# First layer of a two-layer graph network: number row and phases in PSUM, node sums added behind the keys, ScalarE's products first in its turn, and the rounding of the angles on ScalarE

## The chip, the cores and the metric

The kernel runs on one core of a Trainium2 chip. The metric is the device time of one execution in microseconds (us). The kernel before takes 9845.34 us, the median of three runs.

## What is computed

Two message-passing layers over 12500 nodes of 128 channels and 400000 edges, sorted by their target node. Cut to what matters here, the first layer is:

```python
rel_t = last_update[src] - t
rel_t_enc = cos(rel_t[:, None] * time_w[None, :] + time_b)     # 32 phases per edge
e = (concat([rel_t_enc, msg]) @ We)                            # 96 -> 128, two heads of 64
alpha = sum(q_all[dst] * (k_all[src] + e), per head) / 8
ex = exp(alpha - segment_max(alpha, dst)[dst])
out = segment_sum((v_all[src] + e) * ex / segment_sum(ex), dst) + x @ Wskip + bskip
x = layernorm(x + out)
```

The second layer sums `edge_weight * x[src]` per target node, multiplies by a matrix and normalizes again. The change does not touch it.

## The kernel before

Edges come in tiles of 128, one per partition. The first layer walks them in 880 *steps* of G = 4 tiles. Every engine runs its own instruction stream, a loop over *turns*: in turn k an engine does a fixed list of *stages*, each for a step that lies ahead by a fixed number. `(ve_stage, 14)` in the list means that turn k does the `ve` work of step k + 14. The order of that list is the order on the engine, written by hand in each `body`; semaphores tie the engines together. Eight turns are a *round*: once per round come the stages that `first_of` guards (the running maximum over the edges of a node). Counted within a round, turn 3 has the forward and backward scan, turn 4 the running maxima and `new`, turn 5 `shift` and the exponentials, turn 6 `keep`. An angle is worked on for two steps at once (BATCH = 2), in the even turns.

One step passes these stages, in this order:

- GpSimd (POOL) gathers keys, values and update time of 512 source nodes (L817) and subtracts the edge times (`rel`, L825).
- ScalarE (ACT), `arg_stage` (L1178): four products of the phases' frequencies with `rel`, written into `feat`.
- VectorE (DVE), `angle(0)` (L1503) adds the phase offsets; `angle(1)` (L1506) adds MAGIC = 12582912, which rounds to a whole number; `angle(2)` (L1508) subtracts it. Then ACT's `sine_stage` (L1167).
- TensorE (PE), `feat_stage` (L955) transposes `feat`; ACT's `featc_stage` (L1161) copies it out of PSUM; PE's `e_stage` (L963) multiplies with `We`.
- DVE, `ve_stage` (L1518) and `ke_stage` (L1523) add `e` to values and keys; `onehotT_stage` (L1530); PE's `q_stage` (L973); DVE's `product_stage` (L1537) and `alpha_stage` (L1544).
- Once per round: PE transposes alpha (L992), DVE scans forward (L1576) and backward (L1583), PE's `small_stage` (L1006) spreads the ends and ACT's `smallc_stage` (L1194) copies them; DVE takes running maxima (L1602 to L1627) and `new` (L1635), PE's `newT_stage` (L1015) transposes it back, DVE's `shift_stage` (L1642) subtracts, ACT's `exp_stage` (L1201) and `dropx_stage` (L1208) exponentiate, DVE's `keep_part` (L1650 to L1658) ends the round.
- ACT, `weigh_stage` (L1154): eight scaled copies of the values; DVE, `onehot_stage` (L1559), compares the target nodes with the row of numbers 0 to 127 (`irow`); PE's `sum_stage` (L982) sums by node; DVE's `sum_stage` (L1670) adds to `acc`.

Before, `agg_ps`, the target of PE's `sum_stage`, has two banks. ACT alternates between two function tables, one for the sine and one for the exponential, so it loads a table twice a round.

Of the kernel before, what the change touches and what calls it, by code (L numbers as in the profile page):

```python
# [49 lines left out]
def build(nc, x, src, dst, attr, weight, node_vec, time_w, time_b, Wq, bq, Wk, bk, Wv, bv, We, Wskip, bskip, W1, b1, out):  # L50
# [36 lines left out]
    with ctx:  # L87
# [3 lines left out]
        def sem(name):  # L91
            return ctx.enter_context(nc.semaphore(name))
# [25 lines left out]
        eps = sb("eps", [P, 1])  # L118
        We1 = sb("We1", [TD + MSG, C])
# [185 lines left out]
        agg_ps = [banks[6 + j][:, 0:HEADS * HB] for j in range(2)]  # L305
        irow_ps, one_ps = banks[7][:, 0:P], banks[7][0:NB, P:P + 1]
        RANKS = SEGMENT * P
# [40 lines left out]
        s_rows0 = sems("s_rows0", 2)  # L348
# [10 lines left out]
        ANG = 3  # L359
# [516 lines left out]
        def _(pe):  # L876
# [99 lines left out]
            def sum_stage(st):  # L976

                pe.wait_ge(s_wv, st.s + 1)
                pe.wait_ge(s_oh, st.s + 1)
                wait(pe, s_acc, st.before(2))  # L980
                for g in range(G):
                    op = pe.matmul(agg_ps[st.k % 2], oh[:, st.k % QS, g, :], wv[:, st.k % 2, g, :, :].rearrange("p h c -> p (h c)"),  # L982
                                   start=(g == 0), stop=(g == G - 1))
                op.then_inc(s_agg, 1)
# [33 lines left out]
            def body(i):  # L1018
                for k in range(UNROLL0):
                    if first_of(k, 5, ROUND):  # L1020
                        at(i, k, (alphaT_stage, 5))
                    at(i, k, (feat_stage, 15), (sum_stage, 1), (q_stage, 14), (e_stage, 15))
                    if first_of(k, 5, ROUND):
                        at(i, k, (small_stage, 5))
                    if first_of(k, 4, ROUND):
                        at(i, k, (newT_stage, 4))
# [92 lines left out]
        def _(act):  # L1119
# [42 lines left out]

            def sine_stage(st):

                act.wait_ge(s_ang, ANG * (st.batch() + 1))
                enc = encodings(st)
                act.activation(enc, enc, ACT.Sin, bias=zero[:, :], scale=-2.0 * PI_BELOW).then_inc(s_enc, 1)  # L1167

            EDGES, group1 = {0: 6, 6: 8, 14: 2}, {}
# [40 lines left out]
            def body(i):  # L1210
                for k in range(UNROLL0):
                    if k in EDGES:
                        groups_stage(mybir.EngineType.Activation, group1, Step(i, k + 18), EDGES[k])
                    sines = [(sine_stage, 16)] if k % BATCH == 0 else []
# [3 lines left out]
                    at(i, k, (featc_stage, 15), (weigh_stage, 2), *sines, (arg_stage, 18), *gaps, *exps, *smalls)  # L1218
# [74 lines left out]
        def _(dve):  # L1293
# [7 lines left out]
            dve.memset(eps[:, :], 1e-5)  # L1301
            dve.memset(run[:, :, :], -BIG)
# [187 lines left out]
            dve.memset(acc[:, :], 0.0)  # L1490


            def angle(n):

                def stage_of(st):
                    a, t = encodings(st), turns[:, :, :]
                    done = ANG * st.batch()
                    if n:
                        dve.wait_ge(s_ang, done + n)
                    else:  # L1500
                        dve.wait_ge(s_arg, st.s + BATCH)
                    if n == 0:
                        op = dve.tensor_tensor(a, a, brow[:, :].unsqueeze(1).to_broadcast([P, BATCH * G, TD]), ALU.add)  # L1503
                    elif n == 1:
                        wait(dve, s_ang, done)
                        op = dve.tensor_scalar(t, a, MAGIC, None, ALU.add)  # L1506
# [49 lines left out]
            def onehot_stage(st):  # L1556
                dve.wait_ge(s_rel0, st.round() + 1)
                wait(dve, s_agg, st.before(QS))
                dve.tensor_tensor(oh[:, st.k % QS, :, :], irow[:, :].unsqueeze(1).to_broadcast([P, G, P]),  # L1559
# [120 lines left out]
            def body(i):  # L1680
                for k in range(UNROLL0):
# [4 lines left out]
                    def once(ahead, *stages):  # L1686
                        return [(stage_of, ahead) for stage_of in stages] if first_of(k, ahead, ROUND) else []

                    at(i, k, *turn[0], (ve_stage, 14), *turn[1], (ke_stage, 14), *turn[2], (block_stage, 0), *once(5, forward_stage),
                       (onehotT_stage, 15), *once(5, backward_stage), (product_stage, 13), *once(4, run_stage, first_stage),  # L1690
                       (onehot_stage, 2), *once(11, rel0_stage), *once(4, col_stage, drop_stage), (alpha_stage, 13), *once(4, new_stage), *once(3, shift_stage),
                       (sum_stage, 0), *once(8, pen_stage), *once(2, keep_part(0), keep_part(1), keep_part(2)))
# [251 lines left out]
```

## Time and profile before

| | |
|---|---|
| median of three runs | 9845.34 us (9844.81 to 9847.26) |
| the profiled execution, its time and its span | 9864.48 us, 9862.8 us |
| span: VectorE, TensorE, GpSimd, ScalarE busy | 87%, 77%, 68%, 52% |
| first layer's loop, one stretch of 300 us: VectorE, TensorE, ScalarE, GpSimd | 276.31, 233.70, 229.49, 221.06 us |
| steps of the first layer in 800 us (3000 to 3800 us) | 150 |

The times under an engine are those in which it executed an instruction. Consecutive instructions on DVE and ACT overlap by some 0.06 to 0.10 us in the records: what one costs its engine is the distance from its start to the next start, not its duration.

### The profile page before, as it was taken

What the parts mean: (1) busy time and instruction counts of PE and PEld (TensorE: products, weight loads), DVE (VectorE), ACT (ScalarE), POOL (GpSimd) and SP (SyncE); (2) the same over time, 40 slices, a digit from 0 to 9 for tenths busy, and PEclk for the clock granted to TensorE, in tenths of its full rate; (3) what the DMA queues carried; (4) which work ended last, traced back from release to release, by engine and by line L of the source; (5) the groups of instructions that cost most, each with busy time, mean ns of one, the idle gap of its engine ahead of it and who ended that gap; (6) DMA issues with size and microseconds to landing.
All of it is one profiled execution on the core that took longest, in us unless ns stands there. A gap on an engine that the chain in (4) does not pass through costs nothing.

```text
span 9862.8 us, 272152 instructions
## 1 busy us (share of the span) xinstructions
PE 7624.6 (77%) x52868; PEld 7101.3 (72%) x52869; DVE 8560.3 (87%) x21301; ACT 5115.0 (52%) x20838; POOL 6708.6 (68%) x6871
## 2 busy tenths in 40 slices
PE   6477777777777777777756777788888888888855
PEld 2477777777777777777756777787888877877754
DVE  5899999999999999999987666799999999999968
ACT  2377777777777777777753333333333333333300
POOL 0477777777777777777745777777777777777720
PEclk8688988888888888898875555688888888888888
DMA  6467666676666666666632222355555555555544
GB/s 191 114 180 178 179 177 177 178 179 178 176 177 180 177 176 177 178 181 177 177 97 69 71 71 71 106 151 147 149 147 149 148 148 149 148 148 149 148 133 116
DMA packets 1631706, 1484.67 MB, mean 151 GB/s; under 512 B 792007, under 2 KB 1363043, under 8 KB 1631203
## 3 DMA queue, kind: packets, MB, share of 16 engines
q1 hardware_dynamic: 1374244, 848.34, 34.3%
q0 software_dynamic: 257088, 632.95, 22.8%
q14 instruction: 335, 2.74, 0.1%
q8 instruction: 39, 0.64, 0.0%
HBM read 1225.51 MB, written 254.87 MB: 150 GB/s over the span
## 4 chain that ended last, share of the span: by engine, by line
issue 25%; DVE 19%; POOL 18%; PE 14%; DMA 7%; ACT 7%; DVEq 6%; SPq 3%; ACTq 2%; POOLq 0%
POOL message_scratch L869 17%; DMA message_scratch<-ohT,idx 6%; PE bank L982 3%; DVE y_all L1537 3%; PE bank L973 3%; ACT arena L1154 2%; DVEq L531 2%; PE bank L955 2%; PE bank L1015 2%; PE bank L963 2%; DVE acc L1670 1%; SPq L728 1%; DVE oh L1583 1%; DVE oh L1576 1%; DVE kve L1523 1%
## 5 line engine op out<-in xcount | busy, mean ns | idle before, releaser
L817 POOL DMA_INDIRECT kv<-kv_scratch,arena x3136 | 3265.7, 1041 | 1236.6 <-issue 837.5
L869 POOL DMA_INDIRECT message_scratch<-ohT,idx x3232 | 3214.2, 994 | 1079.0 <-issue 880.2
L1261 ACT ACTIVATE ohT<-bank,kv 128x128 f32<-128x128 f32 x3232 | 923.9, 369 | 2703.8 <-DMA message_scratch<-ohT,idx 2665.1
L1154 ACT ACTIVATE arena<-arena,weights 128x65 f32<-128x65 f32 x7040 | 1771.6, 337 | 2.4 <-PE bank L982 2.3
L1063 PE MATMUL bank<-acc,oh 128*128 x6464 | 1211.2, 345 | 520.3 <-ACT ohT L1262 514.4
L1063 PEld LDWEIGHTS bank<-acc,oh 128*128 128x128 f32 x6464 | 1054.7, 247 | 627.7 <-issue 625.2
L1077 PE MATMUL bank<-oh,kve 128*128 128x128 f32 x8640 | 1387.7, 321 | 144.7 <-DVE arena L1838 107.8
L982 PE MATMUL bank<-arena,oh 128*128 128x130 f32 x7040 | 1164.1, 318 | 280.8 <-DVE acc L1670 274.8
L1077 PEld LDWEIGHTS bank<-oh,kve 128*128 128x128 f32 x8640 | 1248.0, 227 | 167.8 <-issue 157.3
L982 PEld LDWEIGHTS bank<-arena,oh 128*128 128x128 f32 x7040 | 1048.2, 227 | 362.6 <-issue 295.1
L973 PE MATMUL bank<-arena,ohT 128*128 128x128 f32 x7040 | 1090.6, 306 | 0.0
L973 PEld LDWEIGHTS bank<-arena,ohT 128*128 128x128 f32 x7040 | 1031.3, 225 | 0.3 <-issue 0.2
L1161 ACT ACTIVATE featT<-bank 96x512 f32<-96x512 f32 x880 | 518.3, 589 | 917.0 <-PE bank L955 895.0
L963 PE MATMUL bank<-We,featT 96*128 96x128 f32 x7040 | 979.5, 284 | 18.3 <-ACT featT L1161 18.3
L963 PEld LDWEIGHTS bank<-We,featT 96*128 96x128 f32 x7040 | 914.3, 202 | 21.4 <-ACT featT L1161 20.1
L1178 ACT ACTIVATE feat<-wrow,rel 128x32 f32<-128x32 f32 x3520 | 830.6, 308 | 163.7 <-POOL rel L825 161.2
L1769 DVE TENSOR_TENSOR_SCAN y_all<-bank,y_all,kv 98x512 f32<-98x512 f32 x707 | 900.4, 1274 | 0.2
L955 PE MATMUL bank<-ident,feat 128*96 128x128 f32 x3520 | 610.7, 301 | 311.9 <-ACT feat L1167 297.5
L1828 DVE TENSOR_TENSOR oh<-bank,kv 128x768 f32<-128x768 f32 x720 | 689.5, 958 | 76.3 <-DVE kv L1821 37.5
L1518 DVE TENSOR_TENSOR arena<-kv,bank 128x512 f32<-128x512 f32 x880 | 597.9, 679 | 159.2 <-PE bank L963 103.6
L1045 PEld LDWEIGHTS bank<-ones,featT 98*128 98x128 f32 x3232 | 516.9, 242 | 226.6 <-issue 173.5
L1794 DVE TENSOR_SCALAR oh<-bank,icol 128x512 f32<-128x512 f32 x808 | 605.5, 749 | 74.5 <-issue 35.5
(232 smaller groups left out, 12653.6 us busy)
## 6 DMA issues: line engine op xcount, KB each, us to landing
kve<-message_scratch SPq DMA_DIRECT2D x2160, 129.0 KB
kve<-nodes_scratch SPq DMA_DIRECT2D x880, 256.0 KB
feat<-in_edge_attr_dram SPq DMA_DIRECT2D x880, 96.0 KB
feat<-block_scratch SPq DMA_DIRECT2D x812, 98.0 KB
arena<-q_scratch SPq DMA_DIRECT2D x880, 64.0 KB
message_scratch<-ohT,idx POOLq DMA_INDIRECT x3232
kv<-kv_scratch,arena POOLq DMA_INDIRECT x3136
feat<-in_edge_attr_dram SPq DMA_DIRECT2D x880, 32.0 KB
```

Source lines behind the costliest of these rows:

```text
L817: pool.indirect_dma_start(kv[:, k, g, :], None, kv_d, bass.IndirectOffsetOnAxis(ap=group_rows[:, half, k * G + g, 0:1].bitcast(I32), axis= ...
L869: pool.indirect_dma_start(msg_d, bass.IndirectOffsetOnAxis(ap=idx[:, k, g:g + 1], axis=0), sum_ring[:, k % RING1, g, :], None).then_inc(s_ ...
L955: op = pe.transpose(featT_ps[:, g * P:(g + 1) * P], feat[:, k, g, :], ident[:, :])
L963: op = pe.matmul(e_ps[st.k % 2][:, g * P:(g + 1) * P], featT[:, st.k % 2, g * P:(g + 1) * P], We1[:, :], start=True, stop=True)
L973: op = pe.matmul(q_ps[st.k % 2][:, g * P:(g + 1) * P], ohT[:, r, g * P:(g + 1) * P], qb[:, r, :], start=True, stop=True)
L982: op = pe.matmul(agg_ps[st.k % 2], oh[:, st.k % QS, g, :], wv[:, st.k % 2, g, :, :].rearrange("p h c -> p (h c)"), start=(g == 0), stop=(g ...
L1063: op = pe.matmul(banks[2 + st.k % 2][:, g * P:(g + 1) * P], oht1[:, st.k % RING1, g * P:(g + 1) * P], acc[:, bass.ds(places[g], C)], start ...
L1077: op = pe.matmul(banks[4 + sg.half][:, b * P:(b + 1) * P], mt[:, sg.slot(MT) + b, a, 0:C], seg_oh[:, sg.half, b, a, :], start=(a == 0), st ...
L1154: op = act.activation(wv[:, st.k % 2, g, h, :], vR[:, st.k, g, h, :], ACT.Copy, scale=weights[:, st.k // ROUND, g, st.k % ROUND, h:h + 1])
L1178: op = act.activation(feat[:, k, g, 0:TD], wrow[:, :], ACT.Copy, scale=of[:, g:g + 1])
L1261: act.activation(sum_ring[:, st.k % RING1, g, 0:C], banks[2 + st.k % 2][:, g * P:(g + 1) * P], ACT.Copy, scale=taken[:, st.k, g, 2:3])
L1769: dve.tensor_tensor_scan(ranks[0:NB, st.k % 2, :], one_ps.to_broadcast([NB, G * P]), in_blk[0:NB, st.k % 2, :], since, ALU.mult, ALU.add). ...
```

## The change

Five things, all in the first layer's loop:

1. `irow` and the phase offsets `brow` are copied once into PSUM bank 7 and read from there by `onehot_stage` and `angle(0)`.
2. `angle(1)` leaves DVE. ACT does it, in a new `whole_stage` with bias MAGIC. ANG, the count of DVE's angle stages, is 2.
3. ACT's turn begins with `arg_stage`, for step k + 17 where it was k + 18 at the end; then `whole_stage`, `featc_stage` and the rest. The stages of a round stay at the end of the turn.
4. DVE's `sum_stage` moves from the end of its turn to behind `ke_stage`, the last angle stage behind it, the scans one place back.
5. Both halves of `agg_ps` are now in bank 6, so PE's `sum_stage` waits until DVE has added the previous step, and it moves to the end of PE's turn.

```diff
-        agg_ps = [banks[6 + j][:, 0:HEADS * HB] for j in range(2)]
+        agg_ps = [banks[6][:, j * HEADS * HB:(j + 1) * HEADS * HB] for j in range(2)]
+        brow_ps = banks[7][:, P:P + TD]
...
-        ANG = 3
+        ANG = 2
...
# TensorE
-                wait(pe, s_acc, st.before(2))
+                wait(pe, s_acc, st.s)
...
-                    at(i, k, (feat_stage, 15), (sum_stage, 1), (q_stage, 14), (e_stage, 15))
+                    at(i, k, (feat_stage, 15), (q_stage, 14), (e_stage, 15), (sum_stage, 1))
...
# ScalarE
+            def whole_stage(st):
+                act.wait_ge(s_ang, ANG * st.batch() + 1)
+                act.activation(turns[:, :, :], encodings(st), ACT.Identity, bias=magic[:, :]).then_inc(s_whole, 1)
...
-                    at(i, k, (featc_stage, 15), (weigh_stage, 2), *sines, (arg_stage, 18), *gaps, *exps, *smalls)
+                    at(i, k, (arg_stage, 17), *wholes, (featc_stage, 15), (weigh_stage, 2), *sines, *gaps, *exps, *smalls)
...
# VectorE
+            dve.tensor_copy(irow_ps, irow[:, :])
+            dve.tensor_copy(brow_ps, brow[:, :]).then_inc(s_tab, 1)
...
                     if n:
-                        dve.wait_ge(s_ang, done + n)
+                        dve.wait_ge(s_whole, st.batch() + 1)
                     else:
                         dve.wait_ge(s_arg, st.s + BATCH)
                     if n == 0:
-                        op = dve.tensor_tensor(a, a, brow[:, :].unsqueeze(1).to_broadcast([P, BATCH * G, TD]), ALU.add)
-                    elif n == 1:
-                        wait(dve, s_ang, done)
-                        op = dve.tensor_scalar(t, a, MAGIC, None, ALU.add)
+                        op = dve.tensor_tensor(a, a, brow_ps.unsqueeze(1).to_broadcast([P, BATCH * G, TD]), ALU.add)
...
-                dve.tensor_tensor(oh[:, st.k % QS, :, :], irow[:, :].unsqueeze(1).to_broadcast([P, G, P]),
+                dve.tensor_tensor(oh[:, st.k % QS, :, :], irow_ps.unsqueeze(1).to_broadcast([P, G, P]),
...
-                    at(i, k, *turn[0], (ve_stage, 14), *turn[1], (ke_stage, 14), *turn[2], (block_stage, 0), *once(5, forward_stage),
-                       (onehotT_stage, 15), *once(5, backward_stage), (product_stage, 13), *once(4, run_stage, first_stage),
+                    at(i, k, *turn[0], (ve_stage, 14), (block_stage, 0), (ke_stage, 14), (sum_stage, 0), *turn[1],
+                       (onehotT_stage, 15), *once(5, forward_stage), (product_stage, 13), *once(5, backward_stage), *once(4, run_stage, first_stage),
...
-                       (sum_stage, 0), *once(8, pen_stage), *once(2, keep_part(0), keep_part(1), keep_part(2)))
+                       *once(8, pen_stage), *once(2, keep_part(0), keep_part(1), keep_part(2)))
```

How the streams move is seen best at two places on ACT and one on DVE. First ACT at the end of turn 5 of a round, before: the last of the four products (L1178), then the wait for DVE's `shift`, the exponentials, and the copy of the next turn.

```order
L1178 ACTIVATE feat<-wrow,rel 128x32
L366 REGISTER_ALU [waits s_shift]
L1201 ACT_TABLE_LOAD
L1201 ACTIVATE weights<-shifted,zero 128x64 [waits s_wv]
L366 REGISTER_ALU [waits s_drop]
L1208 ACTIVATE drop<-drop,zero 128x16 [waits s_keep]
L517 ISA
L517 TENSOR_LOAD walk_rows
L1159 REGISTER_ALU
L1161 ACTIVATE featT<-bank 96x512 [waits s_e,s_feat]
```

The same place now (the products' line is L1185, the exponentials' L1208 and L1215): behind the exponentials comes the first of the four products of turn 6.

```order
L368 REGISTER_ALU [waits s_shift]
L1208 ACT_TABLE_LOAD
L1208 ACTIVATE weights<-shifted,zero 128x64 [waits s_wv]
L368 REGISTER_ALU [waits s_drop]
L1215 ACTIVATE drop<-drop,zero 128x16 [waits s_keep]
L1181 REGISTER_ALU
L1185 REGISTER_ALU [waits s_feat,s_rel]
L1185 REGISTER_ALU
L1185 ISA
L1185 ACTIVATE feat<-wrow,rel 128x32
```

What moved: the products that DVE's next `angle(0)` waits for (semaphore `s_arg`) stood ahead of the wait for `s_shift` and of the table load, and now stand behind both. ACT at the end of turn 3, before: a product, then the copy of the scans' ends.

```order
L1178 ACTIVATE feat<-wrow,rel 128x32
L1194 ACTIVATE small<-bank 128x64 [waits s_first,s_small]
L1159 REGISTER_ALU
L1161 ACTIVATE featT<-bank 96x512 [waits s_e,s_feat]
L1150 REGISTER_ALU [waits s_ex]
L1154 ACTIVATE arena<-arena,weights 128x65 [waits s_agg,s_kve]
```

And now:

```order
L1156 ACTIVATE arena<-arena,weights 128x65 x7
L1201 ACTIVATE small<-bank 128x64 [waits s_first,s_small]
L1181 REGISTER_ALU
L1185 REGISTER_ALU [waits s_feat,s_rel]
L1185 REGISTER_ALU
L1185 ISA
L1185 ACTIVATE feat<-wrow,rel 128x32
```

What moved: the products of turn 4 now follow the copy that waits for PE (`s_small`), which itself waits for DVE's backward scan. DVE at the start of turn 6, before (L1503 to L1523 are the angles, values and keys):

```order
L1503 TENSOR_TENSOR feat<-feat,brow 128x8x32 [waits s_arg]
L366 REGISTER_ALU
L1517 REGISTER_ALU [waits s_wv]
L1518 REGISTER_ALU [waits s_e]
L1518 REGISTER_ALU
L1518 ISA
L1518 TENSOR_TENSOR arena<-kv,bank 128x8x64
L1499 ISA
L1506 TENSOR_SCALAR arena<-feat 128x256 [waits s_ang]
L1523 ISA [waits s_prod]
L1523 TENSOR_TENSOR kve<-kv,bank 128x512
```

And now, from the values on (L1526 values, L1531 keys, L1678 the node sums, L1516 the last angle stage; ahead of it L1514, `angle(0)`, is still first and still waits for `s_arg`):

```order
L1526 TENSOR_TENSOR arena<-kv,bank 128x8x64
L533 ISA
L533 TENSOR_LOAD walk_rows
L1531 ISA [waits s_prod]
L1531 TENSOR_TENSOR kve<-kv,bank 128x512
L1673 REGISTER_ALU
L1678 ISA [waits s_acc,s_keep,s_agg]
L1678 SCALAR_TENSOR_TENSOR acc<-acc,keep,bank 128x65
L1678 ISA
L1678 SCALAR_TENSOR_TENSOR acc<-acc,keep,bank 128x65
L1510 REGISTER_ALU
L1516 SCALAR_TENSOR_TENSOR feat<-arena,feat 128x8x32 [waits s_whole]
```

What moved: the rounding (L1506) is gone, the two node sums stand behind the keys, and the last angle stage behind them.

## Rows read from the trace of the kernel before

**Rows 1.** The page: span, busy times, and the group of the value stage

```profile
span 9862.8 us, 272152 instructions
...
PE 7624.6 (77%) x52868; PEld 7101.3 (72%) x52869; DVE 8560.3 (87%) x21301; ACT 5115.0 (52%) x20838; POOL 6708.6 (68%) x6871
...
L1518 DVE TENSOR_TENSOR arena<-kv,bank 128x512 f32<-128x512 f32 x880 | 597.9, 679 | 159.2 <-PE bank L963 103.6
```

**Rows 2.** Busy time by engine, 3000 to 3300 us (span, busy (count), clock, DMA)

```profile
3000.00:3300.00 300.00, 233.70 (x1726) 220.96 (x1727) 276.31 (x648) 229.49 (x804) 221.06 (x232) 0.90 0.69 179
```

**Rows 3.** Groups of instructions by line and shape, 3000 to 3800 us

```profile
L817 POOL DMA_INDIRECT kv<-kv_scratch,arena x532 | 553.4, 1040 | 214.3 <-issue 141.9 <-DVE kve L1523 70.2 <-DMA kv<-kv_scratch,arena 2.1
...
L1518 DVE TENSOR_TENSOR arena<-kv,bank 128x512 f32<-128x512 f32 x150 | 101.9, 680 | 28.7 <-PE bank L963 19.7 <-issue 7.6
L1559 DVE TENSOR_TENSOR oh<-irow,rel 128x512 f32<-128x512 f32 x149 | 101.1, 679 | 0.0
...
L1503 DVE TENSOR_TENSOR feat<-feat,brow 128x256 f32<-128x256 f32 x75 | 31.6, 421 | 29.1 <-ACT feat L1178 25.8 <-issue 3.3
...
L1506 DVE TENSOR_SCALAR arena<-feat 128x256 f32<-128x256 f32 x75 | 22.7, 303 | 0.0
```

**Rows 4.** Timeline of DVE, backward scan to the end of turn 3

```profile
2981.07 1.21 DVE L1583 TENSOR_TENSOR_SCAN oh<-oh 16x512 f32<-16x512 f32 x1
...
2982.78 0.67 DVE L1559 TENSOR_TENSOR oh<-irow,rel 128x512 f32<-128x512 f32 x1
2983.39 0.67 DVE L1544 TENSOR_REDUCE alpha<-y_all 128x8 f32<-128x512 f32 x1
2983.98 0.45 DVE L1670 SCALAR_TENSOR_TENSOR acc<-acc,keep,bank 128x65 f32 x2
```

**Rows 5.** Timeline of ACT, the copy in turn 3

```profile
2983.65 0.22 ACT L1194 ACTIVATE small<-bank 128x64 f32<-128x64 f32 x1 [1.10 <-PE bank L1006]
```

**Rows 6.** Timeline of ACT, turn 5 to turn 6

```profile
2994.46 0.94 ACT L1178 ACTIVATE feat<-wrow,rel 128x32 f32<-128x32 f32 x4
2995.42 1.28 ACT L1201 ACT_TABLE_LOAD   x1
...
2997.17 0.57 ACT L1161 ACTIVATE featT<-bank 96x512 f32<-96x512 f32 x1
```

**Rows 7.** Timeline of DVE, turn 5 to turn 6

```profile
2994.00 0.21 DVE L1642 TENSOR_TENSOR shifted<-alpha,bank 128x64 f32<-128x64 f32 x1
2994.13 0.47 DVE L1670 SCALAR_TENSOR_TENSOR acc<-acc,keep,bank 128x65 f32 x2
2995.44 0.42 DVE L1503 TENSOR_TENSOR feat<-feat,brow 128x256 f32<-128x256 f32 x1 [0.84 <-ACT feat L1178]
```

**Rows 8.** Timeline of ACT, the products one round later

```profile
3037.44 0.94 ACT L1178 ACTIVATE feat<-wrow,rel 128x32 f32<-128x32 f32 x4
```

**Rows 9.** Timeline of DVE, `shift` one round later

```profile
3036.08 0.21 DVE L1642 TENSOR_TENSOR shifted<-alpha,bank 128x64 f32<-128x64 f32 x1
```

**Rows 10.** Timeline of PE, `newT` in both rounds

```profile
2990.02 1.06 PE L1015 MATMUL bank<-ident,oh 16*128 16x16 f32 x8 [1.01 <-DVE oh L1635]
...
3032.09 1.89 PE L1015 MATMUL bank<-ident,oh 16*128 16x16 f32 x8 [2.45 <-DVE oh L1635]
```

**Rows 11.** Timeline of ACT, turn 6

```profile
2997.65 2.02 ACT L1154 ACTIVATE arena<-arena,weights 128x65 f32<-128x65 f32 x8
2999.68 1.28 ACT L1167 ACT_TABLE_LOAD   x1
...
3001.39 0.94 ACT L1178 ACTIVATE feat<-wrow,rel 128x32 f32<-128x32 f32 x4
```

**Rows 12.** Timeline of DVE, turns 6 and 7

```profile
2996.28 0.69 DVE L1518 TENSOR_TENSOR arena<-kv,bank 128x512 f32<-128x512 f32 x1 [0.42 <-PE bank L963]
...
3001.55 0.69 DVE L1518 TENSOR_TENSOR arena<-kv,bank 128x512 f32<-128x512 f32 x1 [0.17 <-issue]
...
3004.94 0.46 DVE L1670 SCALAR_TENSOR_TENSOR acc<-acc,keep,bank 128x65 f32 x2
```

More of the change, by code:

```diff
@@ L118, in build @@
         eps = sb("eps", [P, 1])
+        magic = sb("magic", [P, 1])
         We1 = sb("We1", [TD + MSG, C])
@@ L347, in build @@
         s_seg = sems("s_seg", MT // SEGMENT)
-        s_rows0 = sems("s_rows0", 2)
+        s_rows0, s_whole = sems("s_rows0", 2), sem("s_whole")
         s_segi, s_acc1 = (sem(n) for n in ("s_segi", "s_acc1"))
@@ L1167, in sine_stage @@
                 act.activation(enc, enc, ACT.Sin, bias=zero[:, :], scale=-2.0 * PI_BELOW).then_inc(s_enc, 1)
-            EDGES, group1 = {0: 6, 6: 8, 14: 2}, {}
+            EDGES, group1 = {0: 7, 7: 8, 15: 1}, {}
             def arg_stage(st):
@@ L1212, in body @@
                     if k in EDGES:
-                        groups_stage(mybir.EngineType.Activation, group1, Step(i, k + 18), EDGES[k])
-                    sines = [(sine_stage, 16)] if k % BATCH == 0 else []
+                        groups_stage(mybir.EngineType.Activation, group1, Step(i, k + 17), EDGES[k])
+                    wholes, sines = ([(stage_of, 16)] if k % BATCH == 0 else [] for stage_of in (whole_stage, sine_stage))
                     gaps = [(gap_stage, 7)] if first_of(k, 7, ROUND) else []
@@ L1301, in _ @@
             dve.memset(eps[:, :], 1e-5)
+            dve.memset(magic[:, :], MAGIC)
             dve.memset(run[:, :, :], -BIG)
@@ L1490, in _ @@
             dve.memset(acc[:, :], 0.0)
+            dve.tensor_copy(irow_ps, irow[:, :])
+            dve.tensor_copy(brow_ps, brow[:, :]).then_inc(s_tab, 1)
+            dve.wait_ge(s_tab, 3)
             def angle(n):
```

## The prediction

> **What bounds the kernel now.** I read the page first: DVE is busy for 87% of the span, the next engine, PE, for 77% [rows 1]. A stretch of the first layer shows the same more sharply: DVE 276.31 of 300 us, PE 233.70, ACT 229.49, POOL 221.06 [rows 2]. So the first layer is DVE's, with gaps. A turn takes 800 / 150 = 5.33 us [rows 3], a round of eight turns 42.67 us, and the 880 steps [rows 1] are 110 rounds, some 4690 us: 1 us per round is worth 110 us.
>
> The groups by line say where DVE's gaps are. In the 150 turns the value stage L1518 stood idle for 28.7 us, mostly for PE's `e`, and `angle(0)` (L1503) for 29.1 us, mostly for ACT's products (L1178) [rows 3]. That is 57.8 / 18.75 = 3.08 us per round. The timeline shows that these gaps are not spread out: after turn 5 DVE is through at 2994.13 + 0.38 = 2994.51 and starts `angle(0)` at 2995.44, just when ACT's products end (2994.46 + 0.94) [rows 6, 7]. After turn 3 DVE does not wait. The question is thus what stands on ACT ahead of those products, now and after the change. DVE has 3.08 us of waits to win back per round, and POOL would allow it: it waits for DVE for 70.2 us per 800 [rows 3], 3.7 us per round.
>
> **The change, part by part.**
>
> *PSUM operands.* The value stage already reads a PSUM tensor and an SBUF tensor of 128x512 and takes 680 ns; the comparison L1559 takes 679 with both in SBUF [rows 3]. I take 0 for both operands moved.
>
> The Trainium skill speaks against it: "VectorE: DVE Perf Modes", section "The TRN2 errata", gives VectorE a fixed 120 cycles from PSUM against 58 from SBUF. By it 1.5 instructions per turn would each cost 62 cycles at 0.96 GHz more, an estimated 85 us in all. The row shows 1 ns of it, so the row decides.
>
> *Rounding.* L1506 has 303 ns [rows 3]; less the overlap of 0.07 (L1559 at 2982.78 lasts 0.67, its follower starts at 2983.39 [rows 4]) it costs DVE 0.23 us, four times a round: -0.9 us. Its wait is now on ACT, whose instruction of the same size as the sine comes some 0.9 us after `angle(0)` started; DVE needs 0.34 + 2 x 0.60 + 0.38 = 1.9 us to get to the last angle stage, so that handover is covered.
>
> *Order of PE and the node sums.* PE's sum for step k + 1 now waits for DVE's sum of step k, 1.9 us into DVE's turn, and must be there for the next turn's sum, 4.8 us later. It takes 1.1 to 2.1 us. Free. Its gain: `e` comes ahead of the sum and no longer waits for the end of DVE's previous turn, so L1518's waits, 28.7 / 18.75 = 1.53 us per round, go.
>
> *Products behind the stages of a round.* This is the part that decides. ACT executes in order, and the products of turn 4 and of turn 6 move behind waits that they stood ahead of.
>
> Turn 3 to 4: the backward scan ends at 2981.07 + 1.21 = 2982.28 [rows 4]. ACT's copy, which needs PE's `small` on those scans, starts at 2983.65 and takes 0.22 [rows 5]. Today nobody waits for that: the products are done. After the change they take another 0.94 + 0.04, so `angle(0)` can start 2.57 us after the scan's end. DVE meanwhile has two instructions, comparison and reduction, 0.61 + 0.59 (starts 2982.78, 2983.39, 2983.98 [rows 4]): 1.2 us. Stall +1.4 us, where now there is none.
>
> Turn 5 to 6: today the order is products, exponentials, copy. From the table load at 2995.42 to the next instruction at 2997.17 are 1.75 us [rows 6]. Without the products ahead of it the load could start at 2994.46; `shift` is done at 2994.21 [rows 7]. Exponentials until 2996.21, products until 2997.15, `angle(0)` at 2997.19. DVE, whose sums no longer stand at the end of the turn, is through at 2994.13: a stall of 3.05 us. One round later the products started at 3037.44, and DVE was behind `shift` (at 3036.08 + 0.13) at 3036.21 [rows 8, 9]: 3037.44 + 1.75 + 0.98 - 3036.21 = 3.96 us. The difference is PE's `newT`: 1.06 us after 1.01 us of idling, 1.89 us after 2.45 [rows 10], and ACT waits for the transpose behind it. After the change PE is idle longer ahead of `newT`, since its sum of turn 4 starts 1.9 us into DVE's turn and takes 1.1, while `new` ends with the turn, near 5.3, so I take 3.7, nearer to the second.
>
> Turn 7 to 0: ACT's work from one `angle(0)` to the products two turns on. Angle 0.47, new rounding 0.41, copy, weighing, table load and sine 2997.17 to 3001.39 = 4.22 [rows 6, 11], products 0.87, copy 0.49, weighing 1.92, products 0.98: 9.36 us. DVE: 0.34, then 2996.28 to 3001.55 less the 0.17 idle and the 0.23 removed, then 3001.55 to 3004.94 and 0.38 more [rows 12]: 8.98 us. Stall +0.4 us (0 to 1.0, since the register loads of the group numbers stand ahead of those products and were covered so far). The pairs without a table load are some 1.3 us shorter on ACT: no stall.
>
> The sum per round: -3.08 (all of today's waits of L1503 and L1518) - 0.9 + 1.4 + 3.7 + 0.4 = +1.5 us; times 110 rounds +165 us. The sum is against the profiled execution's own 9864.48 us; the median 9845.34 is 0.2% below it, and since only differences enter I put them on the median: **10010 us**. With the ends of each term, +0.4 (3.05, 0) to +2.4 (3.96, 1.0) per round, this case's own range is 9890 to 10110.
>
> A second price stands in the table load: the row has 1.28 us, and the exponential follows at once [rows 6]. The Trainium skill ("ScalarE: Activation LUTs", "What ACT_TABLE_LOAD costs") has 2.66 us for a switch, drain included. By it the stall behind turn 5 would be an estimated 1.4 us longer, 150 us in all; the row excludes it.
>
> **The rivals.**
>
> *The offload pays, 17%.* ACT comes to the products early enough because it has slack elsewhere (229.49 of 300 us busy [rows 2]). Then DVE saves 0.9 us and L1518's waits of 1.53, 2.4 us per round: 9580 us, or 9700 if half is given back. It decides if the stalls of turns 3, 5 and 7 together stay under 3.08 + 0.9 = 4.0 us; I have 5.5. Against it: the slack of ACT lies in waits for PE's transpose and for DVE's `shift`, and it cannot be used ahead of them in an in-order queue.
>
> The Trainium skill ("Perfetto Trace Analysis", "Optimizing Scalar/DVE Operations") states that if DVE is saturated, offloading some work to Scalar may make sense. By that rule, this rival.
>
> *The stalls eat just what is saved, 11%.* They come to 4.0 us instead of 5.5: 3.05 behind turn 5 (PE's `newT` always at 1.06 us), nothing behind turn 7, and 0.9 of the 1.4 behind turn 3 because the scans, one place back in DVE's list, leave DVE more to do behind them than I count. 9825 to 9865 us, no measurable change.
>
> *The single bank, 4%.* PE's sum, chained to DVE's sum of the same turn, comes late for the next: if DVE waited 0.4 us in each turn, 880 x 0.4 = 350 us, less the 0.9 + 1.53 us per round: 9930. It decides when adding, handing over and summing take over 4.8 us; with PE at its slow pace they take 0.4 + 2.1 + 0.2.
>
> **The numbers.** My case holds 68%, the rest as above. What a measurement of this kernel can tell from no change is 0.2%, 20 us. Slower by more: 72%; within: 11%; faster: 17%. The range from 9810 to 10110 leaves out most of the first rival and a little above.
>
> **What the profile would show.** Right: DVE's `angle(0)` (L1514) idle for ACT's products (L1185) for over 4 us per round, in two long gaps behind turns 3 and 5; L1526 hardly idle for PE; L1678 not idle; L1567 at 0.68 us. The exponentials' table load starting right behind `shift` or ACT's weighing, the products behind it. Wrong, if `angle(0)` waits for less than 3 us per round, if the comparison from PSUM is longer than 0.68, or if L1678 waits for PE.

## The result

The changed kernel takes 10189.1 us (median of 4 runs, 10177.2 to 10198.5), the kernel before 9846.3 us beside it. The ratio is 1.0343, 95% interval [1.0328, 1.0359]: 343 us slower, where the prediction had 165 and its range ended at 10110.

The page of the changed kernel: span, busy times, and the group of `angle(0)`.

```profile
span 10196.8 us, 271665 instructions
...
PE 7673.1 (75%) x52868; PEld 7119.0 (70%) x52869; DVE 8489.0 (83%) x20864; ACT 5305.4 (52%) x21278; POOL 6523.9 (64%) x6871
...
L1514 DVE TENSOR_TENSOR feat<-feat,bank 128x256 f32<-128x256 f32 x440 | 184.3, 419 | 681.9 <-ACT feat L1185 584.1
```

DVE has 71 us less work than in [rows 1] and the span is 334 us longer. In the stretch of [rows 2]:

```profile
3000.00:3300.00 300.00, 221.27 (x1600) 207.71 (x1600) 252.06 (x569) 222.61 (x771) 192.60 (x215) 0.90 0.64 165
```

Every engine is idler than before; no engine has become the bound. The granted clock is 0.90 in both. Groups by line, 3000 to 3800 us, which answer to [rows 3]:

```profile
L819 POOL DMA_INDIRECT kv<-kv_scratch,arena x499 | 495.2, 992 | 277.8 <-DVE kve L1531 147.2 <-issue 126.1 <-DMA kv<-kv_scratch,arena 4.6
...
L1567 DVE TENSOR_TENSOR oh<-bank,rel 128x512 f32<-128x512 f32 x141 | 95.5, 677 | 0.0
L1526 DVE TENSOR_TENSOR arena<-kv,bank 128x512 f32<-128x512 f32 x140 | 95.4, 681 | 9.8 <-issue 7.7
L1531 DVE TENSOR_TENSOR kve<-kv,bank 128x512 f32<-128x512 f32 x140 | 95.0, 679 | 4.3 <-issue 3.3
...
L1678 DVE SCALAR_TENSOR_TENSOR acc<-acc,keep,bank 128x65 f32 x280 | 65.1, 273 | 0.0
...
L1514 DVE TENSOR_TENSOR feat<-feat,bank 128x256 f32<-128x256 f32 x70 | 29.3, 419 | 104.3 <-ACT feat L1185 86.4 <-issue 16.7
```

In 800 us there are now 140 steps, not 150. DVE stood idle ahead of `angle(0)` for 29.1 us in [rows 3] and does for 104.3 now; the value stage (L1526) no longer waits for PE, but still has 9.8 us of gaps, of which 7.7 have no releaser ("issue"). The comparison from PSUM has 677 ns, 679 before. POOL waits for DVE twice as long.

The timeline shows the two long gaps. Behind the scans, turn 3 to 4, all engines in order of start:

```profile
3025.14 1.21 DVE L1591 TENSOR_TENSOR_SCAN oh<-oh 16x512 f32<-16x512 f32 x1
3026.27 0.65 DVE L1567 TENSOR_TENSOR oh<-bank,rel 128x512 f32<-128x512 f32 x1
3026.85 0.66 DVE L1552 TENSOR_REDUCE alpha<-y_all 128x8 f32<-128x512 f32 x1
3027.72 0.22 ACT L1201 ACTIVATE small<-bank 128x64 f32<-128x64 f32 x1 [2.46 <-PE bank L1008]
3028.11 0.96 ACT L1185 ACTIVATE feat<-wrow,rel 128x32 f32<-128x32 f32 x4 [0.17 <-issue]
3029.09 0.42 DVE L1514 TENSOR_TENSOR feat<-feat,bank 128x256 f32<-128x256 f32 x1 [1.58 <-ACT feat L1185]
3029.92 0.69 DVE L1526 TENSOR_TENSOR arena<-kv,bank 128x512 f32<-128x512 f32 x1 [0.41 <-issue]
```

ACT stands idle for 2.46 us, with the products ready to go behind the copy that PE holds up. Behind `shift`, turn 5 to 6:

```profile
3037.66 0.59 ACT L1163 ACTIVATE featT<-bank 96x512 f32<-96x512 f32 x1 [3.95 <-PE bank L957]
3038.15 2.01 ACT L1156 ACTIVATE arena<-arena,weights 128x65 f32<-128x65 f32 x8
3039.34 0.21 DVE L1650 TENSOR_TENSOR shifted<-alpha,bank 128x64 f32<-128x64 f32 x1
3040.18 1.28 ACT L1208 ACT_TABLE_LOAD   x1
...
3041.73 0.29 ACT L1215 ACTIVATE drop<-drop,zero 128x16 f32<-128x16 f32 x1
3041.93 0.94 ACT L1185 ACTIVATE feat<-wrow,rel 128x32 f32<-128x32 f32 x4
3042.90 0.42 DVE L1514 TENSOR_TENSOR feat<-feat,bank 128x256 f32<-128x256 f32 x1 [3.35 <-ACT feat L1185]
```

`shift` ends at 3039.55; the table load starts 0.6 us later, since the copy waited 3.95 us for PE's transpose and the weighing of 2.01 us stands behind it. A third gap is where DVE's and ACT's loops jump back to their heads (each loop body holds 16 turns):

```profile
3005.04 0.67 DVE L1552 TENSOR_REDUCE alpha<-y_all 128x8 f32<-128x512 f32 x1
...
3005.38 0.96 ACT L1185 ACTIVATE feat<-wrow,rel 128x32 f32<-128x32 f32 x4 [0.21 <-issue]
...
3007.39 0.42 DVE L1514 TENSOR_TENSOR feat<-feat,bank 128x256 f32<-128x256 f32 x1 [1.68 <-issue]
```

The products end at 3006.34, and `angle(0)` starts 1.05 us after them: here something else holds DVE, and the row says "issue".

For the sum I averaged DVE's gaps over the 27 to 30 passes of its loop body between 2000 and 4600 us (a pass is two rounds; 880 steps are 55 passes). All in us per pass:

| | length | DVE at work | idle behind the scans | idle behind `shift` | idle at the jump | other idle |
|---|---|---|---|---|---|---|
| before | 85.46 | 78.69 | 0 | 4.06 | 0.89 | 1.82 |
| changed | 91.87 | 77.46 | 3.63 | 6.65 | 2.19 | 1.95 |

6.41 x 55 = 353 us, against 343 measured. The jump itself, from the compare at the end of DVE's body to the first instruction of its head, took 0.53 us before and 2.06 us on average (1.43 to 3.42; 46 jumps between 600 and 4800 us) in the changed kernel; the body has 542 recorded instructions before and 517 now.

### The profile page after: what moved, and what is told of

It reads as the page before. It is cut to its first block, busy times and chain, and to the rows that moved or that the text cites. A ratio compares the mean times of both kernels' runs of the same rounds, so it can differ in the third digit from the quotient of the medians.

```text
span 10196.8 us, 271665 instructions
## 1 busy us (share of the span) xinstructions
PE 7673.1 (75%) x52868; PEld 7119.0 (70%) x52869; DVE 8489.0 (83%) x20864; ACT 5305.4 (52%) x21278; POOL 6523.9 (64%) x6871
## 3 DMA queue, kind: packets, MB, share of 16 engines
q14 instruction: 335, 2.74, 0.1%
## 4 chain that ended last, share of the span: by engine, by line
issue 27%; DVE 21%; POOL 18%; DVEq 8%; DMA 8%; ACT 7%; PE 6%; SPq 2%; ACTq 2%; POOLq 0%
POOL message_scratch L871 17%; DMA message_scratch<-ohT,idx 7%; DVE y_all L1545 4%; DVEq L533 3%; DVE ohT L1538 2%; DVE acc L1678 2%; ACT arena L1156 2%; ACT feat L1185 2%; DVE alpha L1552 1%; PE bank L1008 1%; SPq L730 1%; DVE oh L1591 1%; DVE oh L1584 1%; DVEq L519 1%; DVEq L1526 1%
## 5 line engine op out<-in xcount | busy, mean ns | idle before, releaser
L819 POOL DMA_INDIRECT kv<-kv_scratch,arena x3136 | 3110.4, 992 | 1739.8 <-DVE kve L1531 906.9
L965 PE MATMUL bank<-We,featT 96*128 96x128 f32 x7040 | 1136.1, 311 | 569.6 <-ACT featT L1163 567.6
L965 PEld LDWEIGHTS bank<-We,featT 96*128 96x128 f32 x7040 | 993.4, 218 | 662.4 <-ACT featT L1163 532.9
L984 PE MATMUL bank<-arena,oh 128*128 128x130 f32 x7040 | 1065.7, 299 | 59.3 <-DVE acc L1678 38.5
L984 PEld LDWEIGHTS bank<-arena,oh 128*128 128x128 f32 x7040 | 971.9, 212 | 83.4 <-issue 51.7
L975 PEld LDWEIGHTS bank<-arena,ohT 128*128 128x128 f32 x7040 | 992.9, 218 | 3.3 <-issue 1.6
L1185 ACT ACTIVATE feat<-wrow,rel 128x32 f32<-128x32 f32 x3520 | 832.5, 308 | 190.7 <-POOL rel L827 156.1
L1163 ACT ACTIVATE featT<-bank 96x512 f32<-96x512 f32 x880 | 511.9, 582 | 609.6 <-PE bank L957 605.5
L1514 DVE TENSOR_TENSOR feat<-feat,bank 128x256 f32<-128x256 f32 x440 | 184.3, 419 | 681.9 <-ACT feat L1185 584.1
```

The lines of the kernel that those rows point to most:

```text
L819: pool.indirect_dma_start(kv[:, k, g, :], None, kv_d, bass.IndirectOffsetOnAxis(ap=group_rows[:, half, k * G + g, 0:1].bitcast(I32), axis= ...
L965: op = pe.matmul(e_ps[st.k % 2][:, g * P:(g + 1) * P], featT[:, st.k % 2, g * P:(g + 1) * P], We1[:, :], start=True, stop=True)
L975: op = pe.matmul(q_ps[st.k % 2][:, g * P:(g + 1) * P], ohT[:, r, g * P:(g + 1) * P], qb[:, r, :], start=True, stop=True)
L1185: op = act.activation(feat[:, k, g, 0:TD], wrow[:, :], ACT.Copy, scale=of[:, g:g + 1])
```

## The experiments

Theory A: the loss is ACT's products standing behind the waits of a round. Theory B: it is the rest of the change (single bank, PSUM operands, the handover of the rounding). Theory C: DVE's late jump back takes part of it. In the expectations A is called theory 1, B theory 2, and C theory 3 (by the loop's place in the code) and 3b (by its length).

**The products' place, from both sides.** `a_products_last` is the changed kernel with the products back at the end of ACT's turn; `b_products_first` the kernel before with them first.

```diff
-                    at(i, k, (arg_stage, 17), *wholes, (featc_stage, 15), (weigh_stage, 2), *sines, *gaps, ...
+                    at(i, k, *wholes, (featc_stage, 15), (weigh_stage, 2), *sines, (arg_stage, 18), *gaps, ...
```

> The changed kernel with ScalarE's four products back at the end of its turn (step k + 18), ahead of the copy, the exponentials and the table load of a round; all else of the change stays. Theory 1 (the products stand behind the waits of a round): of the 5.96 us per round that angle(0) waits in the changed kernel, the 1.6 us behind turn 3 go and of the 3.2 us behind turn 5 about 1.7 go (ACT weighs until 0.7 us after shift, the products take 0.94 more); 3.3 us x 110 = 363 us less than the changed kernel: 9830 us, between 9790 and 9880, at the kernel before. Theory 2 (the place of the products does not matter, the time went into the handover of the rounding or the single bank): 10150 to 10190 us, L1514 still waits 5 to 6 us per round.

> The kernel before with only ScalarE's turn changed: products first (step k + 17), everything else as it was. Theory 1: behind turn 3 the products end 2.57 us after the backward scan, DVE has work for 2.09 us there, +0.5 us; behind turn 5 angle(0) starts 1.75 us later, of which 0.4 to 1.1 us are today a wait for e that is then covered, +0.9 us; 1.4 us x 110 = 155 us: 10000 us, between 9950 and 10060. Theory 2: no change, 9846 us within 20.

Measured: 9850.49 us, ratio 1.0001 [0.9991, 1.0011], and 10059.68 us, 1.0207 [1.019, 1.0224]. The place of the products alone is all of the loss in the changed kernel; in the kernel before it costs 204 us. Groups by line of the first, 3000 to 3800 us, and then of the second:

```profile
L1514 DVE TENSOR_TENSOR feat<-feat,bank 128x256 f32<-128x256 f32 x75 | 31.0, 413 | 60.3 <-ACT feat L1185 30.3 <-issue 28.8
```

```profile
L1518 DVE TENSOR_TENSOR arena<-kv,bank 128x512 f32<-128x512 f32 x144 | 98.2, 682 | 10.3 <-issue 7.7 <-PE bank L963 0.7
...
L1503 DVE TENSOR_TENSOR feat<-feat,brow 128x256 f32<-128x256 f32 x72 | 30.6, 425 | 79.4 <-ACT feat L1178 72.5 <-issue 6.9
```

Theory B falls. The first time lies within its expectation (9790 to 9880), the second at the upper end of its own. But the first kernel has less work on DVE than the one before and is no faster: 28.8 us of "issue" in 800 stand ahead of `angle(0)`. By the same count as above, per pass:

| | length | at work | behind the scans | behind `shift` | at the jump | other |
|---|---|---|---|---|---|---|
| a_products_last | 85.33 | 77.05 | 0 | 2.77 | 2.63 | 2.88 |
| b_products_first | 89.15 | 78.74 | 1.35 | 7.01 | 0.57 | 1.48 |

**What makes the jump late: its place in the code?** `a_shift20` and `b_shift110` put 20 and 110 one-element writes ahead of DVE's loop, which move the whole loop.

```diff
+            for n in range(pads):
...
+                eng.memset(to, 0.0)
```

> The changed kernel with 20 instructions of no use (memsets of one element) ahead of DVE's loop, so that its loop lies 20 instructions further in DVE's code. In the traces the instruction queue fetches 8192 bytes at a time; in the kernel before one of these fetches starts about 20 instructions ahead of the jump back and the jump takes 0.53 us, in the changed kernel it starts 0 to 3 instructions ahead and the jump takes 1.6 to 3.0 us, mean 2.07. Theory 3 (the place of the loop in the code costs the time at the jump): jump back to about 0.5 us, DVE then waits for ACT's products until about 1 us earlier than now; 54 jumps x 1.0 to 1.5 us = 55 to 80 us less: 10110 to 10135 us. Rival (the jump is late for another reason, the order of DVE's last instructions): the jump stays at 2 us, 10189 us within 20.

> The kernel before with 110 one-element memsets ahead of DVE's loop, so that the fetch falls on the jump back as it does in the changed kernel. Theory 3: the jump takes 1.6 to 3 us where it took 0.53, and 54 of them cost 55 to 90 us, plus 7 us for the memsets: 9900 to 9945 us. Rival: 9846 to 9855 us, jump at 0.53 us.

Measured: 10188.46 us, 1.0344 [1.0326, 1.0361], jump 2.07 us; 9850.44 us, 0.9999 [0.999, 1.0009], jump 0.53 us. The place does nothing; that theory fell.

**Its length?** `last_pairs` and `last_long` are `a_products_last` with DVE's block numbers read for two turns at once (body 501 instead of 517), or with 20 small writes at the head of its turn 14 (537). `mid` has the products between copy and weighing, `mid_pairs` the block numbers in pairs too.

```diff
-                blocks[st.k] = several(mybir.EngineType.DVE, blk_i[0:1, bass.ds(st.s, 1)], NB - 1)[0]
+                if st.k % 2 == 0:
+                    for j, found in enumerate(several(mybir.EngineType.DVE, blk_i[0:1, bass.ds(st.s, 2)], NB - 1)):
+                        blocks[st.k + j] = found
```

> The changed kernel with the products last and 20 one-element memsets of no use in the body of DVE's loop, at the head of turn 14, where DVE waits for ACT anyway. So far: body of 542 recorded instructions, jump back 0.53 us; body of 517, jump 2.1 to 2.6 us, wherever the loop lies in the code. Theory 3b (the length of the body counts: fetches come some 128 instructions apart from its head, the fifth at 512 to 520, and with 517 it starts as the jump comes): a body of about 537 gives a jump of about 0.53 us; 1.5 to 2 us of DVE's wait there go in each of 54 iterations: 80 to 110 us under 9850, 9740 to 9790 us, up to 60 us more if the memsets aren't covered. Rival (the last instructions of the body, alpha instead of the node sums, make the jump late): 9850 to 9910 us, jump over 2 us.

> The changed kernel with the products last, and the block numbers read into registers for two turns at once: the body of DVE's loop becomes some 15 instructions shorter (about 502, below 512), and half of the register loads between values and keys go. Theory 3b: jump about 0.5 us, 80 to 110 us less, the loads 5 to 10 us: 9730 to 9770 us. Rival: jump over 2 us, 9840 to 9850 us.

> The changed kernel with the products (step k + 18) between the copy out of PSUM and the weighing, ahead of the weighing's 1.9 us and of all waits of a round. Theory 1: the waits of angle(0) behind turn 5, 1.1 to 1.4 us per round with the products last, go; 1.2 x 110 = 130 us less than 9850: 9720 us, between 9690 and 9770. Rival: the weighing comes late for PE's sums, L1678 waits for PE: 9850 us or more.

> Both of the last two together. Theories 1 and 3b together: 9850 - 130 - 100 = 9620 us, between 9570 and 9680. Rival: POOL's gathers become the bound, and only part of it comes: 9680 to 9750 us.

Measured on a chip on which the kernel before itself takes 13101 us: 13509.28, 13465.69, 13176.1 and 13248.31 us, ratios 1.0296 [1.0272, 1.032], 1.0279 [1.0256, 1.0302], 1.0061 [1.0043, 1.0079] and 1.0106 [1.0087, 1.0125]. The same four on another such chip (13166 us): 1.0283, 1.0278, 1.0062, 1.0141. There DVE waits for what the trace calls remote, for 152 us of 800 in `last_long`, which it does not do in the kernels above, so these times price nothing here: `last_long` and `mid` have no time of their own on the other chips. The jumps can be read all the same: 0.55 us at 537 instructions, 0.25 at 501, 1.81 for `mid` at 517. So the jump goes with the length of the body.

The two with the short body again, on a chip on which the kernel before takes 9858.2 us:

> Products last, block numbers read for two turns at once; body of DVE's loop 501 recorded instructions. On a chip where the kernel before takes 9850 us. Theory 3b: jump 0.25 us, DVE's wait there 2.65 us down to about 1.0 (ACT's products), 54 x 1.6 = 90 us less than with the products last alone, the loads 5 to 10: 9740 to 9765 us. Rival (ACT's products end as late as the jump does now): 9830 to 9850 us.

> Products between the copy and the weighing, block numbers in pairs. Theories 1 and 3b together, from 9850: 130 us for the waits behind turn 5 and 90 for the jump, 9630 us, between 9580 and 9690. Rival: POOL's gathers become the bound: 9690 to 9760 us.

Measured: 9842.41 us, 0.9985 [0.9975, 0.9994], and 9826.71 us, 0.9963 [0.9951, 0.9976], the only two versions faster than before, by 0.15% and 0.4%. Both jumps took 0.25 us, and still neither came near its main expectation; the first lies in the range of its rival, by which ACT's products end as late as the jump did. Groups of the first, then of the second, 3000 to 3800 us:

```profile
L1514 DVE TENSOR_TENSOR feat<-feat,bank 128x256 f32<-128x256 f32 x76 | 31.4, 413 | 47.9 <-ACT feat L1185 46.9
```

```profile
L1526 DVE TENSOR_TENSOR arena<-kv,bank 128x512 f32<-128x512 f32 x150 | 101.8, 679 | 40.0 <-PE bank L965 34.7 <-ACT arena L1156 3.3 <-issue 0.9
L1531 DVE TENSOR_TENSOR kve<-kv,bank 128x512 f32<-128x512 f32 x150 | 101.7, 678 | 12.6 <-issue 10.3
...
L1516 DVE SCALAR_TENSOR_TENSOR feat<-arena,feat 128x256 f32<-128x256 f32 x75 | 31.5, 420 | 16.3 <-ACT arena L1168 16.2
L1514 DVE TENSOR_TENSOR feat<-feat,bank 128x256 f32<-128x256 f32 x75 | 30.7, 410 | 5.0 <-ACT feat L1185 4.0
```

The "issue" part of L1514 is gone, but in the first the wait for ACT grew from 30.3 to 46.9 us; in the second `angle(0)` hardly waits, and the same time stands at the value stage (for `e`) and at the last angle stage (for ACT's rounding). Whichever of ACT's stages comes first, another is late. L1531 has 12.6 us of gaps where `a_products_last` has 4.7; on that see the last experiment.

**The parts of the change one by one.** `sbuf_operands` is the changed kernel with both operands in SBUF. `sums_back` is `a_products_last` with the sums, the banks, PE's order and the operands as before. Of the change the rounding is left and, other than its expectation says, DVE's new order: the block number is still read ahead of the keys, the last angle stage stands behind them, and the scans one place back.

```diff
-                        op = dve.tensor_tensor(a, a, brow_ps.unsqueeze(1).to_broadcast([P, BATCH * G, TD]), ALU.add)
+                        op = dve.tensor_tensor(a, a, brow[:, :].unsqueeze(1).to_broadcast([P, BATCH * G, TD]), ALU.add)
```

> The changed kernel with the number row and the phase offsets read from SBUF again. By the rows of L1518 and L1559 (680 and 679 ns) both operands are free: 10189 us within 20. Rival (PSUM reads cost 65 ns more at 1.5 instructions per turn, or wait for PE's writes): 10105 us. Other rival (two SBUF operands slow POOL's gathers, mean 1040 ns before and 992 after): the gathers go back to 1040 ns, but POOL waits for DVE, so no time: 10189.

> Products last, rounding on ScalarE, but the node sums back at the end of the turns of DVE and PE, two banks, scans and PE's order as before, SBUF operands: that is the kernel before with the rounding alone moved. If moving the sums gave the 1.5 us per round of L1518's waits back that I counted, this run is 100 to 165 us slower than the one with products last: 9950 to 10010 us. If it gave nothing, 9850. The body of DVE's loop stays near 517, so the jump stays at 2 us unless the last instructions decide it.

Measured: 10199.15 us, 1.0348 [1.0331, 1.0365]: the operands' place is worth no time that can be told. 9921.25 us, 1.0066 [1.0049, 1.0083]: the rounding moved, in this order, costs 65 us, less than the 100 to 165 expected. Its keys and its `angle(0)`:

```profile
L1528 DVE TENSOR_TENSOR kve<-kv,bank 128x512 f32<-128x512 f32 x148 | 100.2, 677 | 4.4 <-issue 3.3
...
L1511 DVE TENSOR_TENSOR feat<-feat,brow 128x256 f32<-128x256 f32 x73 | 30.9, 423 | 51.4 <-issue 32.5 <-ACT feat L1185 18.8
```

Its body has 518 instructions, its jump takes 2.81 us. Between `sums_back` (1.0066) and `a_products_last` (1.0001) lie the sums behind the keys, PE's order, the single bank and the operands: together they gain 0.6%, some 64 us. Part of it stands at the jump, which is shorter there (2.63 us): DVE idles 2.84 us per pass in its first turn and not 3.49, some 36 us in 55 passes.

**The jump taken out.** `rounding_pairs` is `sums_back` and `change_pairs` the changed kernel, each with the block numbers in pairs.

> The kernel before with the rounding alone on ACT (as sums_back), and DVE's block numbers read for two turns at once, so that DVE's loop body is some 16 instructions shorter. Theory: the 63 us that sums_back lost were the late jump back (2.81 us from the compare to the loop's head there, against 0.53 in the kernel before). With the shorter body the jump is to take about 0.25 us, and 2.3 us less per round of 16 turns, some 54 rounds, is 124 us: 9790 to 9850 us, with the issue part of L1511's idle time (32.5 us in 800) near nothing. Rival: the loss lies in ACT's later products, which wait behind the rounding; then the jump is short and the time stays at 9900 to 9930 us.

> The whole change, ACT's products first as it has them, with DVE's block numbers read for two turns at once, which only shortens DVE's loop body. Theory: behind the loop's edge DVE waits for the later of two, its jump (2.03 us in the changed kernel) and ACT's products (some 0.7 to 0.9 us there). The jump is to take about 0.25 us, the products then end the wait, and 1.1 to 1.3 us less in each of 54 rounds of 16 turns is 60 to 70 us: 10115 to 10135 us. The waits behind turns 3 and 5 stay as they are (1.6 and 3.1 us). Rival: the jump costs nothing in the changed kernel, since the waits for ACT take it up: 10180 to 10200 us.

Measured beside a kernel before at 9842.3 us: 9869.71 us, 1.0031 [1.0018, 1.0043], and 10150.68 us, 1.031 [1.0293, 1.0328]. Both jumps took 0.25 us. By the ratios `rounding_pairs` gains about 34 us on `sums_back`, a quarter of the 124 expected, and `change_pairs` about 32 on the changed kernel, half of its 60 to 70. Timeline of `change_pairs` at its jump, ACT and DVE:

```profile
3077.23 0.96 ACT L1185 ACTIVATE feat<-wrow,rel 128x32 f32<-128x32 f32 x4 [0.21 <-issue]
...
3078.46 0.42 DVE L1514 TENSOR_TENSOR feat<-feat,bank 128x256 f32<-128x256 f32 x1 [0.28 <-ACT feat L1185]
```

DVE now waits for the products there, for 0.28 us, where it stood idle for 1.68 in the changed kernel. Its groups, 3000 to 3800 us:

```profile
L1531 DVE TENSOR_TENSOR kve<-kv,bank 128x512 f32<-128x512 f32 x140 | 95.1, 679 | 13.5 <-issue 9.5
...
L1514 DVE TENSOR_TENSOR feat<-feat,bank 128x256 f32<-128x256 f32 x70 | 29.2, 417 | 90.4 <-ACT feat L1185 89.3
```

L1514 lost 13.9 us of idling, its "issue" part nearly to nothing, but L1531 gained 9.2: the read of the block numbers ahead of the keys (a TENSOR_LOAD) takes 0.62 us for two where it took 0.35 for one, longer than what stands ahead of it covers. So the pairs have a price of their own, and the true one of the late jump in the changed kernel lies above the 32 us. By the passes, the gap behind turn 15 shrank by 1.85 us, and one of 0.5 us ahead of turn 2 went with it: 2.35 us, 129 us in 55 passes, and that is about its upper end. Of `rounding_pairs`:

```profile
L1523 DVE TENSOR_TENSOR arena<-kv,bank 128x512 f32<-128x512 f32 x149 | 101.2, 679 | 26.7 <-PE bank L965 21.0 <-issue 4.0
L1528 DVE TENSOR_TENSOR kve<-kv,bank 128x512 f32<-128x512 f32 x149 | 101.0, 678 | 14.2 <-issue 11.1
...
L1511 DVE TENSOR_TENSOR feat<-feat,brow 128x256 f32<-128x256 f32 x75 | 31.7, 422 | 29.2 <-ACT feat L1185 26.0 <-issue 3.2
```

With a short jump the kernel is still 27 us slower than before: DVE waits for `e` and for the products as in [rows 3]. But L1528 has 14.2 us of gaps where `sums_back` has 4.4. Those 9.8 us in 800 are the pairs' price, an estimated 57 us over the first layer if no other wait would come in their place. So this run does not tell what the moved rounding is worth without them. From the value stage of turn 5 to that of turn 8, in which ACT loads both tables, it takes 16.98 us before and 17.08 in this kernel, though DVE has one rounding less there; counted from the first instruction of each turn, 16.37 and 16.19.

## Why the prediction was wrong

The direction, the two places and the mechanism of the stalls were right. What failed is mainly the credit in the sum, the 3.08 us of waits that were to go, and then the stall behind turn 7: +1.5 us per round forecast, +3.2 found (6.41 / 2). The terms, in us per round:

| term | forecast | found |
|---|---|---|
| waits of today that go | -3.08 | -2.0 |
| rounding leaves DVE | -0.9 | -0.6 |
| stall behind turn 3 | +1.4 | +1.6 |
| stall behind turn 5 | +3.7 | +3.2 |
| stall behind turn 7 | +0.4 | +1.1 |

"Found" of the last three is L1514's idle time per round in the passes; the rows add up to 3.3, the lengths give 3.2. What else L1514, L1526 and L1531 idle there, 0.32 + 0.55 + 0.24 = 1.1 us, is the part of the 3.08 that did not go.

- *Waits that go: the step that failed most.* That L1518's waits, 1.53 us per round, go was argued from their releaser, PE's `e`. For PE they did go. But 0.55 us stay at L1526, mostly with "issue": register work at the head of the stage, four instructions in the last 0.36 us ahead of it. [Rows 3] showed 7.6 us of "issue" at L1518, L1526 has 7.7 now, and I counted them as won. 0.24 are new at L1531: the change also moves the read of the block number from behind the keys to ahead of them, which is in the diff and not in my list of its parts; L1523 had no gap. Another 0.32 stay at L1514 in turns outside the three stalls, most of it in one turn of the pass (0.5 us ahead of turn 2), which the shorter body of `change_pairs` took away.
- *Rounding.* The 0.23 us each are gone from DVE's stream, but all of DVE's work fell by 0.62 per round, not 0.9 (by 0.82 in `a_products_last`). In `rounding_pairs` the work fell by 0.62 and the idle time rose by 0.75, but that holds the pairs' gaps at L1528. The wait for ACT's rounding was called covered; in the changed kernel it is (L1516 has no idle time), and with the products between copy and weighing it is not (16.2 us at L1516 in `mid_pairs_again`). Neither kernel with the rounding moved and the rest left (`sums_back`, `rounding_pairs`) was faster than before; each has a loss of its own beside it, the late jump or the pairs.
- *Turn 3 to 4* was right: 2.74 us from the scan's end (3026.35) to `angle(0)`, forecast 2.57, and DVE covers 1.16 of them.
- *Turn 5 to 6* was right in kind, 0.5 us too large. The example was taken from a transpose at its slower pace. What the load mostly waits for is not `shift` but the copy and the weighing of turn 5, as the row of L1163 shows: over the rounds between 2000 and 4600 us it starts 0.08 us behind the weighing's end and 0.45 behind the end of `shift`, on average.
- *Turn 7 to 0* was mis-sized, 1.1 for 0.4, and the reason was not in the forecast at all: in every second round the stall lies at the loop's jump, and in the changed kernel the jump is later than ACT's products: 2.1 us once a pass, and in the round without the jump 0.03. With the jump short (`change_pairs`) the wait for the products is 0.29 us once a pass, so the forecast's own mechanism gives some 0.15 us per round, not 0.4. Its 0 to 1.0 allowed for register loads on ACT, not for DVE's own jump.
- *Products behind the stages of a round* "is the part that decides": `a_products_last` shows it, with 0 us left of 343. It costs more in the changed kernel (337 us) than in the one before (204). In the passes the difference is mostly behind the scans, 3.63 against 1.35 us, since there DVE's sums no longer stand between the scans and `angle(0)`; behind `shift` products first cost 3.88 us per pass in the changed kernel and 2.95 in the one before.
- *PE's order, the node sums and the single bank* were free, as forecast: L1678 has no idle time. Together they gain up to some 64 us.
- *PSUM operands* were free: 677 ns against 679, and `sbuf_operands` no faster. By the rule quoted from the Trainium skill ("VectorE: DVE Perf Modes", section "The TRN2 errata") it should have been an estimated 85 us faster; the run shows none of that. The table load took 1.28 us again.
- The rivals: that the offload pays needed stalls under 4.0 us per round, and they are 5.9. With the products back at the end the kernel takes 9850 us, not 9580; what the offload is worth without late jump and pairs no run shows. The single bank costs nothing.

Shown: the products' place carries the whole loss; the jump goes with the body's length, not with its place in the code. Argued only: that ACT's chain from PE's `newT` over copy, weighing, table load and exponentials to the sine and products sets the length of turns 5 to 7, from those turns keeping their length within 0.2 us. Open: the exact share of the late jump in the 343 us, roughly between 32 and 129; no kernel here shortened the body at no cost.

## What to carry to other kernels

Work that changes its place in an in-order queue has to be checked against every wait that it now stands behind, in the turns that come once per round too. The products look as if they moved forward, to the head of the list. But the same step's products, which were the last of one turn's steady stages, are now the first of the next turn, and so they moved back, behind the stages that come once per round: they met two waits there, and that cost 337 us of 9846. A gap whose releaser is removed does not vanish; read its second releaser, "issue" above all, before counting it as won. And taking an instruction off the busiest engine is no gain by itself: here the new gaps were as large as the work saved (`a_products_last`, 9850 us).

## What was not expected of the hardware

The jump back to the head of DVE's loop took 0.25, 0.53 or 1.8 to 2.8 us, by the number of recorded instructions in the loop's body (between 600 and 4800 us; the rows with `last_long`, `last_pairs`, `mid` and `mid_pairs` are from the chip that takes 13101 us):

| body | kernels | jump, mean us |
|---|---|---|
| 501, 502 | pairs_again, mid_pairs_again, change_pairs, rounding_pairs, last_pairs, mid_pairs | 0.25 |
| 517, 518 | changed, a_shift20, sbuf_operands, a_products_last, mid, sums_back | 2.06, 2.07, 2.00, 2.63, 1.81, 2.81 |
| 537 | last_long | 0.55 |
| 542 | before, b_shift110, b_products_first | 0.53 |

The pages show what goes with it. The row of the instruction queue (packets, MB, share), the changed kernel, then `change_pairs`:

```profile
q14 instruction: 335, 2.74, 0.1%
```

```profile
q14 instruction: 79, 0.65, 0.0%
```

The kernel before and those with 517 to 542 instructions have 335 packets (337 with the 110 writes of `b_shift110`), those with 501 or 502 have 79, and between 2000 and 4600 us none of 8 KB: the shortest bodies are not fetched again in each pass, the others are, with five packets a pass. These packets come some 128 instructions apart, counted from the loop's head. With 517 instructions the last of them falls on the jump itself (at instruction 512 to 516), with 542 ahead of it (514 to 532); moving the loop in the code by 20 or 110 instructions changed nothing. That the late packet is what holds the jump is argued from this, not shown. So a change that removes a few instructions can make a loop's jump slower, and one that removes a few more can make it shorter than it was. The Trainium skill ("Runtime: NRT & Kernel Launch", section "Instruction fetch mechanics") says that a taken branch whose target isn't in the window already fetched forces a fetch before execution can go on; the traces agree as far as they go: the jump is shortest where no packet comes, and where packets come its cost is not the same for each loop.

The second: with the two operands in PSUM POOL's gathers are shorter, 992 ns against 1050 with them in SBUF, the rest of the kernel being the same. All kernels on chips on which the kernel before takes some 9850 us fall that way, 984 to 994 ns in six with PSUM operands and 1024 to 1081 in six with SBUF. The row of `sbuf_operands`, 3000 to 3800 us:

```profile
L819 POOL DMA_INDIRECT kv<-kv_scratch,arena x494 | 518.6, 1050 | 243.2 <-issue 129.2 <-DVE kve L1531 112.0 <-DMA kv<-kv_scratch,arena 1.8
```

It brought no time, since POOL then waits for DVE instead, 147.2 us where it was 112.0.
